# Flamingo block on Trainium2: the sixth context tile of seven batches goes through the split passes too, and all splits are made in half tiles

## The reference

```
q   = layernorm(x)                              # 8 x 100 x 2048
a   = einsum('bqd,bkd->bqk', q, ctx)            # scores against 722 context rows
c   = einsum('bqk,bkd->bqd', softmax(a), ctx)   # context rows weighted by the scores
x   = x + tanh(g_xattn) * c
w   = (unpack6bit(qweight) - zero) * scale      # 2048 x 2048
out = x + tanh(g_ffn) * (layernorm(x) @ w.T + bias)
```

## Time and profile before

| | us |
|---|---|
| median of 3 runs | 584.66 (582.53 to 585.20) |
| the profiled execution | 582.69 |
| its span in the profile | 580.9 |
| TensorE busy | 568.8 (98%) |
| VectorE / ScalarE / GpSimd busy | 359.0 / 287.7 / 212.5 |
| granted TensorE clock | full over the whole span |

### The profile page before, as it was taken

The page is one execution under the profiler, slowest core; times in us unless marked ns, Lnnn a source line. Parts: engine busy times, 40 slices in busy tenths (PEclk is TensorE's granted clock), DMA queues, the critical chain, the costliest instruction groups (busy, mean ns, idle before and its releaser), DMA issues.

```text
span 580.9 us, 8745 instructions
## 1 busy us (share of the span) xinstructions
PE 568.8 (98%) x3454; PEld 410.1 (71%) x3454; DVE 359.0 (62%) x684; ACT 287.7 (50%) x451; POOL 212.5 (37%) x187
## 2 busy tenths in 40 slices
PE   7989999999999999999999999999999999999997
PEld 6879969968968968977987986655554444444445
DVE  6577717827836836745764773965949755745443
ACT  3667566568567666675775757545332310210000
POOL 3046177169259349339429619801000000000000
PEclk9999999999999999999999999999999999999999
DMA  8999759226837828737747675778626994972321
GB/s 243 273 298 244 223 159 322 68 99 228 256 108 260 249 83 278 255 94 244 258 134 245 217 253 205 248 283 301 203 88 213 218 241 126 208 155 67 88 55 41
DMA packets 40883, 113.69 MB, mean 196 GB/s; under 512 B 19640, under 2 KB 19896, under 8 KB 32226
## 3 DMA queue, kind: packets, MB, share of 16 engines
q1 hardware_dynamic: 40732, 112.32, 63.9%
q10 hardware_dynamic: 110, 0.82, 0.6%
HBM read 89.26 MB, written 19.66 MB: 188 GB/s over the span
## 4 chain that ended last, share of the span: by engine, by line
PE 86%; DVE 6%; DMA 4%; ACT 1%; issue 1%; POOL 0%; SPq 0%; ACTq 0%
PE S L1157 18%; PE S L1047 13%; PE T L1001 9%; PE pv L1157 8%; PE pv L1085 8%; PE S L1085 8%; PE S L1049 7%; PE pv L1001 6%; DMA raw<-in_ctx 4%; PE pv L1098 3%; PE S L1098 3%; DVE xres L775 2%; PE T L1124 1%; DMA xa<-in_x 1%; PE S L1170 1%
## 5 line engine op out<-in xcount | busy, mean ns | idle before, releaser
L503 POOL TENSOR_TENSOR vlo<-raw,vhi 128x2048 fp32r<-128x2048 f32 (+1 forms) x38 | 174.2, 4615 | 55.0 <-ACT vhi L569 55.0
L1047 PE MATMUL S<-khi,qT 128*100 128x362 f32 x512 | 141.4, 357 | 0.0
L1049 PE MATMUL S<-klo,qT 128*100 128x362 f32 x256 | 85.1, 332 | 0.3
L903 DVE TENSOR_TENSOR klo<-T,khi 128x361 fp32r<-128x361 f32 x128 | 65.9, 529 | 25.5 <-ACT khi L558 24.8
L903 DVE TENSOR_TENSOR klo<-pv,khi 128x361 fp32r<-128x361 f32 x128 | 65.2, 526 | 22.4 <-ACT khi L558 21.8
L558 ACT ACTIVATE khi<-T 128x361 fp32r<-128x361 f32 x128 | 58.5, 474 | 35.3 <-PE T L1001 35.1
L569 ACT ACTIVATE vhi<-raw 128x2048 fp32r<-128x2048 f32 (+1 forms) x38 | 72.0, 1909 | 6.9 <-PE S L1085 6.9
L558 ACT ACTIVATE khi<-pv 128x361 fp32r<-128x361 f32 x128 | 58.4, 476 | 28.4 <-PE pv L1001 28.4
L1157 PE MATMUL S<-raw 128*128 128x512 f16 x320 | 71.7, 379 | 0.0
L1047 PEld LDWEIGHTS S<-khi,qT 128*100 128x100 f32 x512 | 67.8, 167 | 0.0
L1001 PE MATMUL T<-ident,raw 128*128 128x128 f32 (+1 forms) x416 | 64.0, 268 | 3.1 <-DMA raw<-in_ctx 3.0
(11 more groups left out here) (129 smaller groups left out, 748.6 us busy)
## 6 DMA issues: line engine op xcount, KB each, us to landing
raw<-in_ctx SPq DMA_DIRECT2D x24, 1024.0 KB, 9.4
raw<-in_L_ffn_qweight SPq DMA_DIRECT2D x16, 768.0 KB, 7.4
raw<-in_ctx SPq DMA_DIRECT2D x12, 840.0 KB, 9.5
rows_scratch<-xres SPq DMA_DIRECT2D x8, 800.4 KB
xres<-in_x SPq DMA_DIRECT2D x8, 800.0 KB
x_scratch<-xres SPq DMA_DIRECT2D x8, 800.0 KB
raw<-in_ctx SPq DMA_DIRECT2D x12, 512.0 KB, 13.3
late<-x_scratch SPq DMA_DIRECT2D x24, 256.0 KB, 4.1
```

Source lines behind the costliest of these rows:

```text
L503: pool.tensor_tensor(vlo[0:r, k, :], raw[0:r, b % 2, t, 0:D], vhi[0:r, k, :].bitcast(F32), ALU.subtract).then_inc(s_vlo, 1)
L903: dve.tensor_tensor(klo[:, slot, 0:GW], T[k][:, 0:GW], khi[:, slot, 0:GW].bitcast(F32), ALU.subtract).then_inc(s_free[k], 1)
L1047: pe.matmul(into[0:R, g, 0:MW], qT[:, h, c, :], khi[:, slot, :], start=(c == 0 and h == 0), stop=False)
L1049: last = pe.matmul(into[0:R, g, 0:MW], qT[:, 0, c, :], klo[:, slot, :], start=False, stop=(c == CH - 1))
```

## The change

Tile 5 of batches 0 to 6 becomes a split tile, and the split is made in two halves of 1024 columns (`SIDES`): for each half one copy by ScalarE, one subtraction by GpSimd, and six passes of TensorE (two banks, three passes each). The semaphores count halves. The tiles go in the order 0 to 5. ScalarE's copies are placed anew: tile 3's stand ahead of `exps(i + 1)`, tile 4's on both sides of `ln1_norm`, tile 5's ahead of the queries; tile 2's of the next batch are two hooks of the scores (before `khi` 5 and 8) in place of one (before 6). VectorE makes one more small piece (`probs_lo`). The last batch's three whole tiles stay. The diff, cut:

```diff
-    HALVED = 5
-    ORDER = [0, 1, 2, 5, 3, 4]
+    HW = D // 2
+    SIDES = range(2)
...
-                for t in (3, 5, 4):
+                for t in range(3, NT):
                     used(b - 2, t)
                     load_ctx(b, t)
...
             def context_lo(b, t):
-                r = ROWS[t]
-                pool.wait_ge(s_vhi, b * HALVED + t + 1)
-                k = (b * HALVED + t) % PAIRS
-                pool.tensor_tensor(vlo[0:r, k, :], raw[0:r, b % 2, t, 0:D], vhi[0:r, k, :].bitcast(F32),
-                                   ALU.subtract).then_inc(s_vlo, 1)
+                for side in SIDES:
+                    rows, k, cols = unit_at(b, t, side)
+                    pool.wait_ge(s_vhi, 2 * (b * NT + t) + side + 1)
+                    pool.tensor_tensor(vlo[rows, k, cols], raw[rows, b % 2, t, cols], vhi[rows, k, cols].bitcast(F32),
+                                       ALU.subtract).then_inc(s_vlo, 1)
...
-                for t in range(PAIRS, halved(i)):
+                for t in range(PAIRS, NT if i < LAST else PAIRS):
                     context_lo(i, t)
...
                 probs(i)
+                contexts_hi(i, 3)
                 exps(i + 1)
+                context_hi(i, 4, 0)
                 if i + 2 < B:
                     ln1_norm(i + 2)
-                context_hi(i, 3)
-                context_hi(i, 4)
-                context_hi(i + 1, 0)
+                context_hi(i, 4, 1)
+                contexts_hi(i, 5)
                 if i + 2 < B:
-                    queries(i + 2)
+                    queries(i + 2, (0, 1))
+                    contexts_hi(i + 1, 0)
+                    queries(i + 2, (2, 3))
...
+                    for side in SIDES:
+                        lo_made(pe, b, t, side)
+                        rows, k, _ = unit_at(b, t, side)
+                        for n in (2 * side, 2 * side + 1):
+                            if first and b >= 1:
+                                pe.wait_ge(s_x1, (b - 1) * NCH + n + 1)
+                            for p, v in ((0, vhi), (0, vlo), (1, vhi)):
+                                if fresh and p == 1 and n == 0:
+                                    written("P", b, f)
+                                last = pe.matmul(pv[n][0:R, :], ph[rows, p, t, :], v[rows, k, n * 512:(n + 1) * 512],
+                                                 start=(first and (p, v) == (0, vhi)), stop=(final and p == 1))
```

More of the change, by code:

```diff
@@ L292, in used @@
             def used(b, t):
[L294 to L299 removed]
+                lo_made(sp, b, t)
+                if b == 0:
+                    sp.wait_ge(s_scores, 1)
             def next_x(b):
@@ L594, in probs, with last_probs @@
             def probs(b):
-                k, u = bank("P", b, 0)
+                for f in range(2):
+                    k, u = bank("P", b, f)
+                    act.wait_ge(s_turned[k], u + 1)
+                    act.activation(ph[:, 0, 3 * f:3 * f + 2, :], T[k][:, 0:2 * R].rearrange("p (t r) -> p t r", r=R), ACT.Copy)
+                    act.activation(ph[0:ROWS[2], 0, 3 * f + 2, :], T[k][0:ROWS[2], 2 * R:3 * R], ACT.Copy).then_inc(s_phi, 1)
+            def last_probs():
+                k, u = bank("P", LAST, 0)
                 act.wait_ge(s_turned[k], u + 1)
@@ L1065, in attend @@
                     fresh = f not in seen
-                    seen.add(f)
                     if fresh:
+                        seen.add(f)
                         pe.wait_ge(s_phi, 2 * b + f + 1)
-                    if t < halved(b):
-                        lo_made(pe, b, t)
-                        k = (b * HALVED + t) % PAIRS
-                        passes = ((0, vhi), (0, vlo), (1, vhi))
-                        if final:
-                            written("P", b, f)
-                            steps = [(a, n) for n in range(NCH) for a in range(3)]
-                        else:
-                            steps = [(a, n) for a in range(3) for n in range(NCH)]
-                        for a, n in steps:
-                            p, v = passes[a]
-                            if (a, n) == (2, 0):
-                                written("P", b, f)
-                            if first and a == 0 and b >= 1:
-                                pe.wait_ge(s_x1, (b - 1) * NCH + n + 1)
-                            last = pe.matmul(pv[n][0:R, :], ph[0:r, p, t, :], v[0:r, k, n * 512:(n + 1) * 512],
-                                             start=(first and a == 0), stop=(final and a == 2))
-                            if final and a == 2:
@@ new lines, in attend @@
+                    if t == 5 and b == LAST:
+                        written("P", b, f)
+                    if b == LAST and t >= PAIRS:
+                        p = pT[0:ROWS[5], :] if t == 5 else E[0:ROWS[t], t - 3, 0:R]
+                        for n in range(NCH):
+                            if first:
+                                pe.wait_ge(s_x1, (b - 1) * NCH + n + 1)
+                            pe.matmul(pv[n][0:R, :], p, raw[0:ROWS[t], b % 2, t, n * 512:(n + 1) * 512],
+                                      start=first, stop=False)
+                        continue
```

103 lines of the change are left out of this document (40 added, 63 removed).

## The result

The changed kernel takes 591.14 us (median of 6 runs, 589.16 to 593.98) against 584.83 of the kernel before beside it (6 runs, 582.53 to 585.20): ratio 1.0117, 95% interval 1.0086 to 1.0149. It is slower by 1.2%, 6.3 us. The forecast was slower, 588.3; the range held the time. The profiled execution took 589.16 us against 582.69, span 587.3 us against 580.9.

The account below looks back on a forecast made before the run. TensorE was taken to bound the kernel. The terms -2.5 + 1.3 + 2.2 + 2.7 gave +3.7 us: 586.4 on the profiled execution, 588.3 on the median, with a range of 582.5 to 592.0.

Parts of the forecast that it names:

- its own case: Whole kernel: the prediction's main account, 586 to 590.5 us, given a chance of 0.50.
- the third rival: GpSimd's half subtraction costs far more than half, 2.5 us: +9.3 us, 594 in all; chance 0.06.
- Batches 0 to 4: Part of the term for batches 0 to 5: each gains 0.42 us, six together -2.5 us.
- The 0.2 us taken as free: Start of the next scores: some 0.2 of TensorE's 0.44 us wait falls into time its weight load is idle anyway.
- Batch 7's scores: TensorE waits for `klo` behind a held VectorE piece and a later second weight load: together +1.3 us.
- the held piece: Batch 7's scores: VectorE's first 16-bit piece waits for GpSimd, so TensorE waits 1.1 us for `klo` 16.
- the second load: Batch 7's scores: the second weight load goes out 1.9 us later and TensorE waits 0.2 more.
- `attend(6)`: GpSimd starts 6.4 us into the stage, TensorE waits from tile 3's second half on: +2.2 us.
- `attend(7)`: `unpack(2)` pieces wait for GpSimd's halves, delaying `rows_lo(1, 0)` and TensorE's next row turns: +2.7 us, bounds 0 and 3.
- the whole gain: Rival: TensorE never waits for GpSimd, -4.6 us, 580.1 in all; chance 0.10.
- The cancelling of terms: Rival: a half costs 2.30 us and VectorE's pieces slip in, sum -1.3 to +1.2, 583.4 to 585.9; chance 0.34.

Follow-up runs that it names:

- E3: Changed kernel with the ten unpacking pieces in batch 7's scores placed two `klo` later; 589.97 us, ratio 1.0061 to the kernel before.
- E2: Changed kernel with batch 5's eight small GpSimd instructions behind tile 5's halves, ScalarE's normalising and turned-weight copies following; 590.44 us, ratio 1.0068.
- E1: Changed kernel with VectorE doing `rows_lo(1, 0)` ahead of `unpack(2)` instead of behind it; 588.23 us, ratio 1.0047.
- E7: Changed kernel with GpSimd pausing before batch 7's last tile until `unpack(2)` is done; 589.58 us, ratio 1.0103.
- E5: Changed kernel with GpSimd subtracting only 512 of each half's 1024 columns, leaving part of the result out; 578.42 us, ratio 0.9920.
- E8: Changed kernel with the GpSimd pause of E7 and the edits of E2 and E3; 588.23 us, ratio 1.0074.
- E10: E8 with GpSimd's pause lasting until `unpack(3)` is done; 586.64 us, ratio 1.0064.
- E11: Changed kernel with E2 and E3, both unpackings first, GpSimd pausing before batch 7's tile 1 and doing batch 6's small instructions then; 586.34 us, ratio 1.0037.
- E6: Changed kernel with batch 7's three subtractions made whole, copies and passes staying in halves; 587.47 us in one run.
- E4: Changed kernel with the edits of E1, E2 and E3 together; 588.28 us, ratio 1.0046.
- E9: Changed kernel with all six tiles split but copies, subtractions and semaphores by whole tiles again; 605.60 us, ratio 1.0373.
- E12: E10 with batch 6's small GpSimd instructions moved into its pause; 585.70 us, ratio 1.0023.

## Why the prediction was right, and where its sizes were off

The direction, the places and the mechanisms hold; the sum was +3.7 on the profiled execution and the measured difference is +6.4. The median of 591.14 lies above the 586 to 590.5 that the prediction gave its own case. It is inside the range only because this was drawn up to 592.0 for the third rival, a dearer half, which is not what happened: that part is luck.

1. *Batches 0 to 4*: forecast -0.42 each, measured -0.31 (-1.55 in five; the sixth, batch 5, shares its period with the next term). A half was taken at 2.35 us, with bounds of 2.30 and 2.39; it is 2.37 from one start to the next. GpSimd ended 16.96 us after the start of `attend` (forecast 16.8), TensorE waited 0.40 (0.44). But the sixth split tile cost 2.90, not 2.77: `attend(2)` took 178.01 - 159.52 = 18.49 against 178.81 - 160.19 = 18.62, so 3.43 us of whole tile less 0.13 gained and 0.40 waited leaves 2.90. TensorE's restart behind a wait shows in the 0.48 in place of 0.39 of its first pass. The 0.2 us taken as free at the start of the scores came: 0.22.

2. *Batch 7's scores*: forecast +1.3 over a normal batch, measured 46.83 - 45.26 = 1.57. TensorE lost 0.81 to the held piece (forecast 1.1) and 0.73 to the second load (forecast 0.2). GpSimd was done 34.1 us after the start of `attend(5)` where the forecast had 33.5, since its last six halves took 14.45 with the piece that slipped in; the load went out that much later. How much the second wait costs hangs on the load's landing (E3) and is not a fixed price.

3. *`attend(6)`*: forecast +2.2, measured +2.30. GpSimd's start (6.40 us in), its six halves (14.18), the three waits and the stage's 22.10 for 22.0 all came out. E2 confirms the cause: with the start at 2.7 us in, the stage takes 19.14.

4. *`attend(7)`*: forecast +2.7, measured +4.43. This is the term that was mis-sized. The wait itself was right: TensorE sat idle for 2.45 us before 379.35, and the stage was 2.61 longer up to there. How it came about was not quite as told: the forecast had four pieces wait for the end of one half each; in the trace one piece waited for all four halves, 9.31 us, and the others took 0.49. The sum is the same, since both end with GpSimd's last half. (E2 and E3 show the forecast's picture: in E3 four pieces took 2.32, 2.73, 2.67 and 2.65 us, one half each.) What was missing is the price behind the wait: 1.77 us at 1.2 GHz, a term that the sum did not have. E1 and E7, where the longest wait there is 1.13, have no such stretch and 25.1 us for the stage.

The sentence on the Trainium skill ("GPSIMD Engine Reference", section 1: GpSimd shares SBUF interfaces with VectorE, with contention against two-port modes) is borne out in that the pieces contend with the subtractions; that section does not say by how much, and no run here shows in which mode a piece runs. What the runs show is a stop until a subtraction ends and not a slowing: E7's 4.69 us and the 9.31 us here. By the rate of section 3.1 of the same reference in the Trainium skill the estimate for a half was 2.28 us; measured were 2.37 to 2.40. By that estimate six halves end at 162.25 + 13.68 = 175.93, before the 176.14 at which TensorE wanted the last one, and its wait of 0.40 us in each batch would have been gone.

Of the rivals, the whole gain is nearly what E5 shows: -4.2 us in the span for -4.6, at a subtraction of 1.3 us. The cancelling of terms needed 2.30 us for a half and pieces that slip in; one of them did (326.63), and it was worth nothing, since the next was held. A half of 2.5 us was not there; and by the prediction's own sum the batches lose from 2.42 us a half on, not from 2.40.

## What to carry over

- When a helper engine's list grows, don't ask for its share of the period but for the stages where it starts late or where its work runs up against another engine's: here 0.3 us gained in each ordinary batch stood against 8 us lost in the three stages at the end, where no further stage hides the helper.
- Put instructions of one engine that are held beside another's long ones into that engine's pauses, and follow every release that the pause delays, loads included: E2, E8, E10 and E11 each removed one wait and met the next one soon after.
- Price a long wait of TensorE with what follows it: a few microseconds at half the clock nearly doubled one here.

## What the runs showed of the hardware

- **A VectorE `TENSOR_SCALAR` against a subtraction.** One on 128 x 512 uint16, 0.5 us alone, took 9.31, 4.69 and 4.41 us beside GpSimd's subtractions (three in a row took 7.9 in E2), and each held one ended within 0.4 us of a subtraction's end. At some boundaries between two subtractions it got in (326.8 after; 371.0 in E6; 368.6 in E8), at others it did not (369.9, 372.3 and 374.6 after; 374.3 in E7). With whole subtractions it is the same. What decides this stays open. It is not a matter of 16 bits: the float32 one on 128 x 2048, 1.27 us alone, took 2.45 and 3.37 us in E10. And it goes both ways: the subtraction right behind one that got in took 2.6 to 2.7 us in place of 2.4 (16 bits), or 3.3 (float32). VectorE's other work of the same time (`klo`, the residual, the statistics) shows no such wait: the four statistics in `attend(7)` took 2.47 us, beside subtractions, against 2.46 in the feed-forward part without them.
- **The subtraction's cost.** 512 columns 1.30 us, 1024 columns 2.40, 2048 columns 4.59 in a row: about 1.10 us for each 512, and 0.2 for the instruction.
- **The clock behind a wait.** In the last attention, after waits on the weight load of 2.73 (E6), 2.83 (E8), 2.88 (E3) and 3.30 us (after, E4) the granted clock was 0.50 for 3.4 us, and with one of 4.72 (E2) for 6.8 us, from 1.3 us before its end on. After waits of 1.10 and 1.13 (E7, E1), of up to 1.84 (E9) and of 1.73 in the feed-forward part (before) it stayed at full. After 2.63 and 3.03 there (E11, E12) it fell for 3.4. But E10's 4.05 at 388.07, and E9's three waits in each `attend`, had none behind them, so the length of the wait alone does not decide. Nor is it the same in every execution: one of E3's ten (586.22 us) had a mean clock of 1.000, so no such stretch at all.
